# One transformer tower layer on Trainium2: the experts' bias as three bf16 rows of a 32-row tile instead of two rounded float32 rows of a 64-row tile

## The reference, cut to what matters

```python
H = gelu(xf @ W1 + b1)                       # 2048 x 256
probs = softmax(H @ Wg + bg)                 # 2048 x 8
assign = argmax(probs)
for e in range(8):
    y = H @ Wd[e] + bd[e]                    # 2048 x 64
    out += where(assign == e, probs[:, e] * y, 0)
```

## Time and profile before

| what | value |
|---|---|
| median of 3 runs | 117.33 us (115.77 to 124.94) |
| the profiled execution's own time | 116.27 us |
| its span, first to last instruction | 114.5 us |
| mean granted TensorE clock | 0.947 of full |
| busy: PE, PEld, DVE, ACT, POOL | 99.9, 70.1, 90.5, 68.8, 58.0 us |

### The profile page before, as it was taken

One profiled execution on the slowest core, in us unless ns is written; L12 is line 12 of the kernel. 1 busy time (PEld: TensorE's weight loads), 2 busy tenths in 40 slices (PEclk: granted clock), 3 DMA queues, 4 the chain that ended last, 5 costly groups with the idle time before them and its releaser, 6 DMA issues.

```text
span 114.5 us, 1858 instructions
## 1 busy us (share of the span) xinstructions
PE 99.9 (87%) x651; PEld 70.1 (61%) x651; DVE 90.5 (79%) x229; ACT 68.8 (60%) x117; POOL 58.0 (51%) x101
## 2 busy tenths in 40 slices
PE   5831999997799999979988989999999999999940
PEld 2240778525732399864988758877876667577620
DVE  0347999999999998699988299959969239599971
ACT  1903567968999999999991628633582667501000
POOL 7598999889999401705349605166506000000750
PEclk9999999999855999995999999999999999999996
DMA  4999900000000000000000000000000000000033
GB/s 87 238 199 378 398 16 6 0 3 0 0 0 0 0 9 0 3 0 0 0 0 6 0 0 0 0 0 6 0 3 0 0 0 6 0 0 0 0 101 82
DMA packets 3449, 4.40 MB, mean 38 GB/s; under 512 B 2288, under 2 KB 2544, under 8 KB 3312
## 3 DMA queue, kind: packets, MB, share of 16 engines
q1 hardware_dynamic: 3136, 3.91, 11.4%
q10 hardware_dynamic: 304, 0.38, 1.8%
HBM read 3.76 MB, written 0.52 MB: 37 GB/s over the span
## 4 chain that ended last, share of the span: by engine, by line
PE 67%; ACT 9%; DVE 7%; DMA 7%; POOL 5%; issue 2%; SPq 0%; POOLq 0%
PE pair L1033 21%; PE pair L922 10%; PE pair L908 9%; DMA ids<-x 7%; PE pair L956 7%; PE bank L995 5%; ACT bell L454 3%; PE pair L1040 3%; PE hid_pair L1006 3%; PE pair L884 3%; POOL bdp L364 3%; PE bank L978 2%; PE hid_pair L1016 2%; DVE pair L783 2%; ACT bell L450 2%
## 5 line engine op out<-in xcount | busy, mean ns | idle before, releaser
L783 DVE COPY_PREDICATED pair<-later,pair 128x256 f32<-128x256 int32 (+3 forms) x30 | 12.3, 409 | 5.9 <-PE pair L1033 5.2
L956 PEld LDWEIGHTS pair<-amps,bell 128*128 128x128 f32 x128 | 15.2, 197 | 1.1 <-DVE amps L694 0.9
L371 POOL TENSOR_SCALAR var_eps<-mean_var 128x4 f32<-128x4 f32 x8 | 3.3, 408 | 24.7 <-DVE mean_var L719 24.5
L956 PE MATMUL pair<-amps,bell 128*128 128x64 f32 x128 | 15.4, 280 | 0.0
L908 PE MATMUL pair<-onehot,w1p 128*128 128x512 f32 x32 | 10.2, 489 | 2.7 <-DVE w1p L622 2.7
L922 PE MATMUL pair<-h,w_sb 128*64 128x512 f32 x40 | 11.9, 755 | 0.0
L704 DVE SCALAR_TENSOR_TENSOR bell<-bell,scale_w,wave 128x512 f32<-128x512 f32 x16 | 11.6, 788 | 0.2 <-ACT wave L460 0.2
L387 POOL TENSOR_TENSOR angle<-picked,prob 128x256 f32<-128x256 f32 x3 | 1.8, 613 | 18.3 <-DVE prob L807 18.3
L1033 PE MATMUL pair<-wd_high,H_high 128*128 128x512 f32 x32 | 10.8, 419 | 0.0
L908 PEld LDWEIGHTS pair<-onehot,w1p 128*128 128x128 f32 x32 | 7.7, 246 | 4.8 <-DVE w1p L622 2.8
L1033 PE MATMUL pair<-wd_low,H_high 128*128 128x512 f32 x32 | 9.9, 391 | 0.0
(11 more groups left out here) (160 smaller groups left out, 228.5 us busy)
## 6 DMA issues: line engine op xcount, KB each, us to landing
ids<-x SPq DMA_DIRECT2D x2, 512.0 KB, 6.6
posb<-positions SPq DMA_DIRECT2D x1, 768.0 KB, 9.6
wd_sb<-wd SPq DMA_DIRECT2D x1, 512.0 KB, 10.6
out<-angle SPq DMA_DIRECT2D x4, 128.0 KB, 2.0
st_sb<-state SPq DMA_DIRECT2D x1, 328.0 KB, 9.8
bd_sb<-bd ACTq DMA_DIRECT2D x2, 128.0 KB, 6.7
w_sb<-w SPq DMA_DIRECT2D x1, 256.0 KB, 8.2
posb<-positions SPq DMA_DIRECT2D x1, 256.0 KB, 8.2
```

The costliest lines, as they stand in the source:

```text
L783: return dve.copy_predicated(held[:, :, 0:n, 0, 0:D], repeat(later[:, g, 2 * h + rows.start:2 * h + rows.stop, first:first + n], 3, D), he ...
L956: mm = pe.matmul(bank[g][:, b * D:(b + 1) * D], bell[:, g, at:at + P], amps[:, g * GB + b, :], start=(s == 0), stop=(s == NS - 1))
```

## The change

The bias becomes three bfloat16 parts (first, second, rest), on three neighbouring partitions, and the product that adds it uses 3 rows, partitions 0 to 2 for jj = 0 and 64 to 66 for jj = 1, with ones in bfloat16.

- One transfer brings the first row of `bd` to all 128 partitions of `bd_sb`, where two of 64 rows each brought 64 rows.
- ScalarE makes `bd_first`, the bias rounded to bfloat16, as the first of its main list, ahead of `distances(1)`; it waits for the transfer there. The old copy between `field_out(2)` and `load_gelu` is gone.
- GpSimd makes the parts in `bias_parts`, right behind its tables and ahead of `inv_std(0, 0)`: two flags per partition (the column `value` is the partition's number modulo 64; the flags say whether it is at least 1 and at least 2), then five instructions over 128 x 512, each waiting for the one before. Partition 0 gets the first part, partition 1 the second, partition 2 and those behind it the rest. `bias_rest` is gone.

```diff
--- before.py
+++ after.py
@@ -115,8 +115,13 @@
 
         embp = [sb(f"embp{i}", [V, D + NL], BF16) for i in range(3)]
         embr = [sb(f"embr{i}", [V, D + NL]) for i in range(2)]
-        bdp = sb("bdp", [P, NE * D], F32R)
-        ones = sb("ones", [P, P], F32R)
+        bd_first = sb("bd_first", [P, NE * D], BF16)
+        bd_second = sb("bd_second", [P, NE * D], BF16)
+        bd_rest = sb("bd_rest", [P, NE * D])
+        bd_cut = sb("bd_cut", [P, NE * D])
+        bdp = sb("bdp", [P, NE * D], BF16)
+        after = sb("after", [P, 2])
+        ones = sb("ones", [P, P], BF16)
         warm = sb("warm", [P, T], BF16)
         shapes = sb("shapes", [P, NB, NL])
         taps = sb("taps", [P, NB, K3])
@@ -295,7 +300,7 @@
             pool.memset(gate_w[:, :, :], 0.0).then_inc(s_gate_pad, 1)
             pool.memset(h1[:, :, 0:2], 0.0)
             pool.memset(h1[:, :, 2 + P:], 0.0)
-            pool.memset(ones[:, :].bitcast(F32), 1.0).then_inc(s_cst, 1)
+            pool.memset(ones[:, :], 1.0).then_inc(s_cst, 1)
             link(pool.memset(decay[:, :, :], 1.0))
             pool.memset(decay[:, :, 0:1], 0.0).then_inc(s_ones_decay, 1)
             slot = iter(range(32))
@@ -358,12 +363,17 @@
             pool.tensor_tensor(drive_tab[:, :], upper[:, 0, :], upper[:, 1, :], ALU.add).then_inc(s_tables, 1)
             pool.wait_ge(s_tables, 1)
 
-            def bias_rest(part, after):
+            def bias_parts():
 
                 pool.wait_ge(s_bd_part, 1)
-                pool.tensor_tensor(bdp[part, :], bd_sb[part, :], bdp[part, :].bitcast(F32),
-                                   ALU.subtract).then_inc(s_bd_split, 1)
-                pool.wait_ge(s_bd_split, after)
+                for k in range(2):
+                    ins = pool.tensor_scalar(after[:, k:k + 1], col("value"), k + 1.0, None, ALU.is_ge)
+                link(ins)
+                link(pool.tensor_scalar(bd_cut[:, :], bd_first[:, :], after[:, 0:1], None, ALU.mult))
+                link(pool.tensor_tensor(bd_rest[:, :], bd_sb[:, :], bd_cut[:, :], ALU.subtract))
+                link(pool.tensor_copy(bd_second[:, :], bd_rest[:, :]))
+                link(pool.tensor_scalar(bd_cut[:, :], bd_second[:, :], after[:, 1:2], None, ALU.mult))
+                pool.tensor_tensor(bdp[:, :], bd_rest[:, :], bd_cut[:, :], ALU.subtract).then_inc(s_bd_split, 1)
 
             def inv_std(n, g):
 
@@ -390,11 +400,9 @@
                     repeat(prob[:, g].rearrange("p (h b) -> p b h", h=2), 3, D), ALU.mult))
                 pool.tensor_tensor(result[:, g], scaled[:, g], h_b[:, g], ALU.add).then_inc(s_result, 1)
 
+            bias_parts()
             inv_std(0, 0)
             inv_std(0, 1)
-            pool.wait_ge(s_rstd[0], 2)
-            bias_rest(slice(32, D), 1)
-            bias_rest(slice(D + 32, P), 2)
             inv_std(0, 2)
             inv_std(1, 0)
             inv_std(0, 3)
@@ -407,8 +415,7 @@
         @block.scalar
         def _(act):
             act.dma_start(sm[:, :], small).then_inc(ld["small"], 16)
-            for half in range(2):
-                act.dma_start(bd_sb[half * D:half * D + D, :], bd[0:D]).then_inc(ld["bd"], 16)
+            act.dma_start(bd_sb[:, :], repeat(bd[0], 0, P)).then_inc(ld["bd"], 16)
             act.wait_ge(ld["small"], 16)
             act.activation(spar[:, 0:1], col("log_re"), ACT.Exp).then_inc(s_sexp, 1)
             act.activation(spar[:, 1:2], col("log_dt"), ACT.Exp).then_inc(s_sexp, 1)
@@ -518,6 +525,8 @@
                     act.wait_ge(s_logit, g - 1)
                 act.copy(gate_sb[:, g % 2, :], gate_rows).then_inc(s_gcopy, 1)
 
+            act.wait_ge(ld["bd"], 16)
+            act.copy(bd_first[:, :], bd_sb[:, :]).then_inc(s_bd_part, 1)
             distances(1)
             conv1_out(0)
             distances(2)
@@ -555,8 +564,6 @@
             cosine(3)
             normalise(0, 1)
             field_out(2)
-            act.wait_ge(ld["bd"], 32)
-            act.copy(bdp[:, :], bd_sb[:, :]).then_inc(s_bd_part, 1)
             load_gelu()
             transposed_out(0, 1)
             normalise(0, 2)
@@ -1036,13 +1043,13 @@
 
             def expert_bias(h, jj):
 
-                rows = slice(jj * D, (jj + 1) * D)
+                rows = slice(jj * D, jj * D + 3)
                 pe.matmul(pair[h][:, jj, :], ones[rows, :], bdp[rows, :], start=True, stop=False)
 
             def experts_high(g, h):
 
                 if g == 0:
-                    pe.wait_ge(s_bd_split, 2)
+                    pe.wait_ge(s_bd_split, 1)
                     pe.wait_ge(s_wd_split, 1)
                     pe.wait_ge(s_ha, 2 * h + 2)
                 else:
```

## The result

The changed kernel takes 121.2 us in the median (120.9 to 121.36), the kernel before 117.36 in the same comparison: a ratio of 1.0391, 95% interval 1.0326 to 1.0457. It is slower, by some 4.6 us going by the ratio, and lies outside the forecast range of 115.0 to 119.3. The profiled execution took 121.36 us; its span is 119.5, and 114.5 before, which makes 5.0. Single executions of the kernel before ranged from 115.77 to 124.94 us, the long ones at a lower granted clock where it is on record, so every ratio compares the fast executions alone, and a profile is read for its stretches.

The account below looks back on a forecast made before the run. It took engine handovers, with DVE's order leading to `field(2)`, to bound the kernel before 68.58, and TensorE alone after. Terms 0 + 2.2 - 0.6 - 0.7 = +0.9 us on 116.27 gave 117.2 us, range 115.0 to 119.3.

Parts of the forecast that it names:

- What bounds the kernel: Before 68.58 engines hand over to each other, afterwards only TensorE counts; DVE delay before 44 reaches `field(2)` less 0.33 us.
- The transfer and the first copy: At the start, one transfer and ScalarE's copy ahead of `distances(1)` fit into its 0.80 us wait: 0, bounds -0.4 and +0.5.
- GpSimd's work by itself: Behind GpSimd's tables, flags and five wide instructions take 5.8 us from 38.65 to 44.5, within its idle hole, so free.
- R3: Rival: GpSimd is held back instead of DVE between 38 and 48, +0.3 in all, 116.6 us; chance 0.18.
- DVE's loss: From 38.65 to 43.95 GpSimd's new work slows DVE's angles and product by 2.5 us, +2.2 after 0.33 us of slack.
- R2: Rival, slower: each wide GpSimd instruction costs DVE its full length, 5.0 us instead of 2.5; 119.6 us, chance 0.17.
- What goes at 58 to 61: The old copy and GpSimd's two subtractions leave, so `inv_std(0, 2)` starts sooner: -0.6 us, bounds -0.7 and 0.
- The bias products: On TensorE, eight pairs each save 0.085 us through a bf16 weight load: -0.7 us, bounds 0 and -1.5.
- The sum: All terms, 0 + 2.2 - 0.6 - 0.7, make the kernel +0.9 us slower, at 117.2 us.

Follow-up runs that it names:

- experiment 4: The kernel before with one wait added on TensorE alone: `field(1)` also waits for the first rstd; ratio 1.0487 to the kernel before.
- experiment 6: The kernel before with only the type of the bias rows and the ones changed to bfloat16, still 64 rows per product; ratio 0.9928.
- experiment 3: The kernel before with two wide subtractions, or three wide one-input instructions, added on GpSimd behind its tables; these cost DVE 1.81 and 1.57 us.
- experiment 1: The changed kernel without the bias parts on GpSimd, ScalarE copying the bias straight to bf16; ratio 0.9916 to the kernel before.

## Why the prediction was wrong, point by point

- *What bounds the kernel.* Right as far as it went: DVE from 38 to 44 leads, and a delay there reaches the end. The sentence that failed is "A delay of DVE before 44 therefore arrives at `field(2)` less 0.33 us." It arrived doubled, 3.2 us at L733 and 6.4 at `field(2)`. I followed DVE's order and forgot that `field(1)` waits for the same product, on an engine whose granted clock fell to 0.50 behind such a wait (experiment 4). The rows had a hint that I did not use: the earlier trace rows show `field(2)` at 4.23 us, for work that takes 3.68 at the full clock.
- *The transfer and the first copy, 0.* Right: the copy ran at 12.09 and the distances at 12.61, earlier than before.
- *GpSimd's work by itself, 5.8 us, ending at 44.5.* It ran from 36.85 to 47.04, 10.2 us. It began early because the tables had ended early (36.76, where it was 38.57); in experiment 6 they ended at 38.95, in experiment 4 at 36.78, with the same GpSimd instructions up to there. Each instruction was longer than forecast, above all the two scales of bf16 into f32, 2.50 and 1.88 us where I took 0.8; how much of that is waiting behind DVE the rows do not tell. The late end cost nothing more, since L381 behind it still waited 1.57 us for DVE's moments; so R3 did not decide either.
- *DVE's loss, 2.5 us.* The mechanism was right, the size too small: 9.07 - 5.82 = 3.25 against the kernel before, or 3.45 against undisturbed groups. Both rates were low, 0.90 against 0.77 and 0.52 against 0.33 per instruction (experiment 3). They came from narrower instructions. That narrowness is the reason was not tried; and of the one-input tables that I counted, L354 ran from 34.37, with none of the L704 beside it until 34.81, and L661's 0.19 us went to the two-input tables although the one-input L353 ran beside it from 32.57.
- *The term that was missing.* The lower clock behind TensorE's wait ahead of `field(1)`: some 2 to 3 us of the result by the runs with 16 zeros, 3.1 of the 6.4 us at `field(2)`. Wait and clock together, with DVE on time, cost 4.9% in experiment 4. In R2 I wrote that TensorE would stand idle longer, and gave it no price. R2 came nearest with 119.6, for the wrong reason: it charged DVE 5.0 us.
- *What goes at 58 to 61, -0.6.* Right: 6.4 became 5.8.
- *The bias products, -0.7.* Right: from L1002 to TensorE's last product 40.14 us, where it was 40.89, so -0.75; the pair 0.32, the weight load 90 ns.
- *The sum.* 6.4 - 0.6 - 0.75 = 5.05, and the spans differ by 5.0.

That the clock falls after an idle stretch is also what the Trainium skill says (TensorE: Matmul & The Clock Gate, "HAM oscillation — how this bites in real kernels"). The changed kernel and experiment 4, with 0.50 behind waits of 2.81 and 3.50 us, agree with its sense. In experiment 1 the clock was at 0.79 over the stretch of `field(1)` with no wait ahead of it, so idle gaps alone do not account for these rows. What else decides was not tried.

## What to carry to other kernels

An engine's idle hole is only free if the engine that it slows down has one too: before moving work to GpSimd, look at what DVE runs in that stretch, and price each wide instruction by a run of its own. When a delay makes TensorE wait, price the products behind the wait at the lower clock, and not just the wait, and all that TensorE does until the clock is back; here that was everything up to `field(2)`. Products of zeros in that place can be worth their time. And split a change into its parts: here the bf16 type gave 0.7% by itself, at the edge of what the runs can tell, and making three parts on GpSimd cost 4.8%.

## What the runs showed of the hardware that was not expected

- A wait of TensorE of 3.50 us, with nothing added on another engine, cost the kernel 4.9%: `field(1)` took 7.06 us at a granted clock of 0.50, against 3.76 at 1.00 in the kernel before.
- Sixteen products of zeros ahead of it made it 3.68, though they made it start 2.6 us later; the granted clock came back from 0.50 to 1.00 while they ran.
- A scale of 128 x 512 from bf16 into f32 on GpSimd took 1.87 us at the least and 2.50 in the changed kernel, a copy from f32 into bf16 0.73 and 1.49, a subtraction in f32 1.3 to 1.6. DVE was at work beside each of them, so none of these is GpSimd's own time alone.
- The weight load of the ones takes 90 ns in bf16 (92 in 64 rows) and 183 in float32r. The products stream the same 512 columns in 64 rows or in 3; a pair costs 0.32 us in either, and its type decides.
- GpSimd's tables end between 36.2 and 37.3 in most profiles and at 38.57 and 38.95 in two (the kernel before and experiment 6), with the same GpSimd instructions up to there. In the kernel before, one instruction on a single column (L335) took 6.61 us beside three of DVE's long multiplications in a row (L646); in the changed kernel three small ones took some 2.2 us each there. What decides it was not tried.
